# A 13-tile closing of a third half layer, with finer copies and new places, in a product-interaction MLP kernel

## The reference, cut to what matters

```python
sparse_embed = emb_tables[field_idx[None, :], x_sparse]   # 1024 x 26 x 64, gathered rows
z = sparse_embed.reshape(B, 26 * 64)
gram = jnp.einsum('bik,bjk->bij', sparse_embed, sparse_embed)
inner = gram[:, iu, ju]                                   # the 325 products of pairs of fields
dnn_in = jnp.concatenate([x_dense, z, inner], axis=-1)    # 13 + 1664 + 325 = 2002 columns
h = jax.nn.relu(dnn_in @ w1 + b1)                         # w1 is 2002 x 2002
out = jax.nn.sigmoid(h @ w2 + b2)
```

## Time and profile before

| | |
|---|---|
| median of 3 runs | 435.78 us (435.40 to 436.06) |
| the profiled execution | 435.87 us, of it the span from first to last instruction 434.1 us |
| TensorE busy | 409.5 us, 94% of the span |
| VectorE, ScalarE, GpSimd busy | 72%, 61%, 53% |
| TensorE's granted clock, mean | 0.992 of full speed |
| HBM read | 77.55 MB, 179 GB/s |

### The profile page before, as it was taken

One profiled execution on the slowest core, in us unless ns is written; L12 is line 12 of the kernel. 1 busy time (PEld: TensorE's weight loads), 2 busy tenths in 40 slices (PEclk: granted clock), 3 DMA queues, 4 the chain that ended last, 5 costly groups with the idle time before them and its releaser, 6 DMA issues.

```text
span 434.1 us, 5915 instructions
## 1 busy us (share of the span) xinstructions
PE 409.5 (94%) x1959; PEld 336.8 (78%) x1959; DVE 313.7 (72%) x691; ACT 265.2 (61%) x365; POOL 228.7 (53%) x215
## 2 busy tenths in 40 slices
PE   8769999899799999999999899989999999999996
PEld 8647878788678787888877778868888888778884
DVE  3374876586949987895998799995484986984432
ACT  3442363577996896967478595694952686353310
POOL 5777777877777877787787778781000000000000
PEclk9998999999899999999999999999999999999999
DMA  5787777775469776469699656686477157578400
GB/s 137 200 266 168 234 190 226 218 245 129 110 157 232 199 216 166 120 150 215 177 206 308 149 111 168 166 279 193 114 221 282 47 192 184 161 228 281 136 0 0
DMA packets 29454, 77.95 MB, mean 180 GB/s; under 512 B 8480, under 2 KB 8488, under 8 KB 29424
## 3 DMA queue, kind: packets, MB, share of 16 engines
q1 hardware_dynamic: 22768, 70.75, 51.6%
q0 software_dynamic: 6656, 6.83, 13.4%
HBM read 77.55 MB, written 0.00 MB: 179 GB/s over the span
## 4 chain that ended last, share of the span: by engine, by line
PE 52%; DVE 13%; POOL 12%; ACT 10%; issue 7%; DMA 4%; SPq 1%; DVEq 0%; ACTq 0%; POOLq 0%
PE ps L588 15%; PE ps L600 15%; PE ps L590 15%; POOL z L480 12%; PE ps L548 6%; ACT w_hi L668 3%; ACT pair_v L692 2%; DVE weighed L886 2%; DVE tail L844 2%; DVE w_lo L782 2%; DMA z<-in_L_rec_emb_tables_dram,idx 2%; DMA w_raw<-in_L_rec_w_dram 2%; ACT pair_u L689 2%; DVE square L825 1%; PE ps L534 1%
## 5 line engine op out<-in xcount | busy, mean ns | idle before, releaser
L480 POOL DMA_INDIRECT z<-in_L_rec_emb_tables_dram,idx x208 | 227.7, 1095 | 65.2 <-issue 62.5
L588 PE MATMUL ps<-w_hi,x_hi 128*128 128x502 f32 (+1 forms) x512 | 206.5, 403 | 7.9 <-DVE x_lo L790 4.6
L590 PE MATMUL ps<-w_lo,x_hi 128*128 128x502 f32 (+1 forms) x480 | 188.4, 393 | 0.0
L668 ACT CAST w_hi<-w_raw 128x1002 fp32r<-128x1002 f32 x128 | 128.7, 1033 | 49.4 <-PE ps L600 32.7
L600 PE MATMUL ps<-w_hi,x_lo 128*128 128x502 f32 (+1 forms) x480 | 139.8, 393 | 1.0 <-DVE x_lo L854 1.0
L588 PEld LDWEIGHTS ps<-w_hi,x_hi 128*128 128x128 f32 x512 | 97.2, 190 | 33.1 <-DVE x_lo L790 5.9
L600 PEld LDWEIGHTS ps<-w_hi,x_lo 128*128 128x128 f32 x480 | 90.3, 190 | 19.7 <-DVE x_lo L854 1.6
L590 PEld LDWEIGHTS ps<-w_lo,x_hi 128*128 128x128 f32 x480 | 91.6, 191 | 16.4
L782 DVE TENSOR_TENSOR w_lo<-w_raw,w_hi 128x1002 fp32r<-128x1002 f32 x60 | 70.1, 1198 | 26.3 <-ACT w_hi L668 26.1
L778 DVE TENSOR_TENSOR w_lo<-w_raw,w_hi 128x502 fp32r<-128x502 f32 x60 | 40.8, 680 | 28.7 <-ACT w_hi L668 28.5
L676 ACT CAST x_hi<-ps 128x256 fp32r<-128x256 f32 (+3 forms) x38 | 17.1, 450 | 52.5 <-PE ps L534 52.4
(11 more groups left out here) (51 smaller groups left out, 205.4 us busy)
## 6 DMA issues: line engine op xcount, KB each, us to landing
w_raw<-in_L_rec_w_dram SPq DMA_DIRECT2D x112, 501.0 KB
w_raw<-in_L_rec_w_dram SPq DMA_DIRECT2D x24, 250.5 KB
w_raw<-in_L_rec_w_dram SPq DMA_DIRECT2D x8, 438.4 KB
z<-in_L_rec_emb_tables_dram,idx POOLq DMA_INDIRECT x208, 4.4
w_raw<-in_L_rec_w_dram SPq DMA_DIRECT2D x24, 62.6 KB
w2b<-in_L_rec_w_dram SPq DMA_DIRECT2D x1, 501.0 KB, 5.9
w2b<-in_L_rec_w_dram SPq DMA_DIRECT2D x1, 500.0 KB, 7.1
w_raw<-in_L_rec_w_dram SPq DMA_DIRECT2D x8, 50.9 KB
```

The lines of the kernel that those rows point to most:

```text
L480: pool.indirect_dma_start(out=z[:, t % 2, K * f:K * (f + 1)], out_offset=None, in_=emb_rows, in_offset=bass.IndirectOffsetOnAxis(ap=idx[:, ...
L588: nc.tensor.matmul(into(c, t), hi, of_w(w_hi, c, k), start=first, stop=False)
L590: nc.tensor.matmul(into(c, t), hi, of_w(w_lo, c, k), start=False, stop=False)
L668: nc.scalar.copy(high_of(n), raw(n)).then_inc(w_hi_done, 1)
```

## The change

It does these things.

- The third pair's first half (pair 2, half 0) joins `SPLIT`: closed after its 13 z tiles, and its tail becomes one turn behind k 10 of its second half.
- 20 fillers at the start for 29; single fillers behind turns 3 and 98 for two behind turn 33.
- The low parts of weights are made in 4 instructions for the first pair (`W_PARTS`), 2 for the second, 1 for the others; before, 2, 2, 1, 1.
- The pair copies of a tile are four blocks with places of their own, for two; each block has the same instructions for one of the two `par`.
- Indices of the first four fields of the first two tiles are made first, the rest of these in a second round.
- Of tile 2 one block of products less is read by ScalarE and of tile 3 one more, and for tile 7 block 3 in place of block 2 (`BY_ACT`).
- Nearly all events have new places; those that the text speaks of stand below.

```diff
-    PARTS_OF = [(0, 7), (7, FP - 7)]
+    PARTS_OF = [(0, 0, 7), (1, 0, 7), (0, 7, FP - 7), (1, 7, FP - 7)]
...
-    WARM_UP = 29
+    WARM_UP = 20
+    W_PARTS = (4, 2, 1, 1)
...
-    TAIL_AFTER = {(1, 0, 9): [(0, 1)], (1, 0, 11): [(0, 0)], (2, 0, 2): [(1, 0)]}
-    SPLIT = [(1, 0)]
+    TAIL_AFTER = {(1, 0, 9): [(0, 1)], (1, 0, 11): [(0, 0)], (2, 0, 2): [(1, 0)], (2, 1, 10): [(2, 0)]}
+    SPLIT = [(1, 0), (2, 0)]
...
-        ('J', 0): [-1.0, -0.5, 0.0, 1.0, 2.0, 3.5, 5.2, 6.0, 7.5, 10.9, 14.3, 15.8, 18.4, 19.1, 19.2],
-        ('J', 1): [24.5, 26.3, 28.4, 31.5, 33.2, 36.4, 37.2],
-        ('O', 0): [13.4, 23.8],
-        ('G', 0): [25.8, 25.9, 26.6, 26.9],
-        ('R', 0): [27.9],
-        ('X', 0): [29.4],
-        ('O', 1): [27.7, 28.5],
+        ('J', 0): [-1.0, -0.5, 0.0, 1.0, 2.0, 5.2, 6.0, 7.5, 7.9, 10.9, 14.3, 15.4, 18.4, 19.6, 19.8],
+        ('J', 1): [24.0, 26.3, 28.4, 31.5, 33.0, 36.4, 37.2],
+        ('O', 0): [9.0, 16.1, 23.6, 23.6],
+        ('G', 0): [25.8, 25.9, 26.6, 26.7],
+        ('R', 0): [27.2],
+        ('X', 0): [29.8],
+        ('O', 1): [27.7, 27.7, 28.3, 28.5],
...
-        ('G', 2): [40.0, 40.8, 41.2, 41.4],
-        ('X', 2): [44.0],
-        ('T', 4): [44.8, 46.6, 48.5, 52.8],
-        ('T', 5): [53.3, 53.9, 57.2, 59.2],
-        ('X', 5): [70.0],
-        ('X', 7): [102.4],
+        ('G', 2): [40.0, 40.6, 41.1, 42.1],
+        ('X', 2): [45.3],
+        ('T', 4): [44.4, 47.3, 49.2, 53.5],
+        ('T', 5): [52.1, 53.8, 56.7, 58.7],
+        ('X', 5): [78.6],
+        ('X', 7): [99.8],
...
-    WARM = [(33.4, 2)]
+    WARM = [(3.5, 1), (98.5, 1)]
...
-                first, n = PARTS_OF[q]
+                par, first, n = PARTS_OF[q]
...
-            make_rows(slice(0, GROUP), idx_in, 0)
+            make_rows(slice(0, GROUP), slice(0, 2 * ALONE), 0, idx_in, 0)
+            make_rows(slice(0, GROUP), slice(2 * ALONE, FIELDS), GROUP * 2 * ALONE, idx_in, 3)
...
-                    if TURN[PIECE[m][0]][2][0] < GROUP * EARLY_PAIRS:
-                        half = CW[0]
-                        nc.vector.tensor_tensor(low[:, 0:half], raw(n)[at, 0:half], high[:, 0:half], ALU.subtract)
-                        nc.vector.tensor_tensor(low[:, half:], raw(n)[at, half:], high[:, half:],
-                                                ALU.subtract).then_inc(w_lo_done, 1)
+                    part = W_PARTS[TURN[PIECE[m][0]][2][0] // GROUP]
+                    if part > 1:
+                        ends = [HW * j // part for j in range(part + 1)]
+                        for lo, hi in zip(ends, ends[1:]):
+                            last = nc.vector.tensor_tensor(low[:, lo:hi], raw(n)[at, lo:hi], high[:, lo:hi], ALU.subtract)
+                        last.then_inc(w_lo_done, 1)
```

More of the change, by code:

```diff
@@ L175, in product_interaction_mlp_kernel @@
+        ('G', 6): [79.7, 81.3, 87.7, 88.0],
+        ('R', 6): [94.0],
+        ('X', 6): [97.2],
+        ('T', 7): [73.9, 75.1, 78.2, 90.7],
+        ('O', 7): [89.7, 91.0, 91.0, 91.4],
+        ('G', 7): [93.5, 94.5, 95.9, 96.5],
+        ('R', 7): [96.9],
+        ('X', 7): [99.8],
     }
-    WARM = [(33.4, 2)]
+    WARM = [(3.5, 1), (98.5, 1)]
     KINDS = "JTOGRXW"
@@ L487, in _ @@
                 if pair == 1:
-                    pool.wait_ge(idx_done, 2)
+                    pool.wait_ge(idx_done, 3)
                 for q, (first, n, of) in enumerate(JOINT[pair]):
+                    if pair == 0 and first == ALONE:
+                        pool.wait_ge(idx_done, 2)
                     if pair:
@@ L684, in pair_operands @@
                 act.wait_ge(x_hi_done, count("JTX", slices_event(t, first + n - 1)))
-                for par in range(2):
-                    high = x_hi[K * par:K * (par + 1), t % XS, first:first + n, :].rearrange(
-                        "p f (g b) -> p f g b", b=2)
-                    at, to = QUAD // 2 * par + first, FP * par + first
-                    nc.scalar.copy(pair_u[0:K, :, :, at:at + n, :].rearrange(two), high)
-                    if t in ACT_COPIES:
-                        nc.scalar.copy(pair_v[K:2 * K, :, :, to:to + n, :].rearrange(two), high)
-                    last = nc.scalar.mul(pair_v[0:K, :, :, to:to + n, :].rearrange(two),
-                                         high.bitcast(fp32), 0.5)
+                high = x_hi[K * par:K * (par + 1), t % XS, first:first + n, :].rearrange(
+                    "p f (g b) -> p f g b", b=2)
+                at, to = QUAD // 2 * par + first, FP * par + first
+                nc.scalar.copy(pair_u[0:K, :, :, at:at + n, :].rearrange(two), high)
+                if t in ACT_COPIES:
+                    nc.scalar.copy(pair_v[K:2 * K, :, :, to:to + n, :].rearrange(two), high)
+                last = nc.scalar.mul(pair_v[0:K, :, :, to:to + n, :].rearrange(two),
+                                     high.bitcast(fp32), 0.5)
                 last.then_inc(pairs_act, 1)
@@ L746, in _, with make_rows @@
         def _(dve):
-            def make_rows(tiles, loaded, step):
+            def make_rows(tiles, fields, first, loaded, step):
                 dve.wait_ge(loaded, 16)
-                i, w = idx[:, tiles, :], wrap[:, tiles, :]
+                i = idx[:, tiles, fields]
+                n = (tiles.stop - tiles.start) * (fields.stop - fields.start)
+                w = wrap[:, first:first + n].rearrange("p (t f) -> p t f", t=tiles.stop - tiles.start)
                 nc.vector.tensor_scalar(w, i, 0, VOCAB, ALU.is_lt, ALU.mult).then_inc(idx_step, 1)
```

64 lines of the change are left out of this document (28 added, 36 removed).

## The result

The changed kernel took 430.09 us in the median of 4 runs (428.32 to 431.55), the kernel before 435.59 beside it (435.24 to 436.06): a ratio of 0.9864, 95% interval 0.9827 to 0.9902. The forecast was 429.3, within 423.5 to 434.6. The profiled execution took 430.07 us, its span 428.3 for 434.1. Medians and ranges here are of all runs of a kernel; the ratios, each against the kernel before run beside it, leave out a run that is over 1.5% above the fastest of its kernel (one each in experiments 3, 5 and 7).

What follows compares the result with a forecast made beforehand. No one engine was taken to set the time: TensorE has half the chain and is held at a list of waits. 435.87 - 3.0 (up to G(1,0)) - 3.6 (five later waits) = 429.3 us, range 423.5 to 434.6.

Steps and rivals of the forecast that it cites:

- Fillers, 0: At the start: fewer fillers gain 0, since TensorE next waits for tile 1's first copy, behind weights; clock cost taken as 0.
- J(0,5), 2.0 ahead at turn 6: J(0,5) moved from behind turn 3 to behind turn 5: turn 6 starts at 36.0 for 38.0, 2.0 us ahead.
- Quarters, 2.9 off the gathers: First pair's low parts in four instructions: gather excess halves from 5.7, saving 2.9 us at the last gather, bounds 0 and 4.
- J(0,14), no wait: J(0,14) moved within turn 20: its 1.4 us wait for the last gather goes, 3.4 us ahead at turn 21.
- Indices in two rounds: At the start: the first gather comes 0.1 to 0.2 us earlier, nothing on the path by itself.
- ScalarE at turn 30, 3.0 ahead at G(1,0): 81 to 121 us: the tail's wait becomes a wait for ScalarE's copies; 3.0 us ahead at G(1,0).
- Five waits, 3.6: 121 to 430 us: five TensorE waits lose their cause, 2.82 us idle plus 0.165 each for pipelining, 3.6 us.
- The split, its own cost 0: Third pair's first half: four sums kept on ScalarE and added on VectorE are covered, cost 0; without that cover 2.7 us.
- The gathers hold: Rival, 10%: VectorE's instruction length does not delay gathers, the last lands at 80.5, lead 1.6 at G(1,0); 430.7 us.
- More of the list goes: Rival, 17%: as many waits again vanish and the start keeps 2 us more; 423.7 us.
- The lead is given back: Rival, 15%: from 100 to 290 us new places make new waits on ScalarE and VectorE; 433 us.
- ScalarE's order at turn 30: Rival, 8%: if the start gives nothing, turn 30 ends at 121.8, 0.9 late; 437.5 us; decides below 0.7 lead at turn 26.

Runs made afterwards that it cites:

- experiments 3, 5 and 7: 3: kernel before with the start's changes, 431.47 us; 5: that plus split and three tile-6 places, 429.16; 7: changed kernel, T(5) places back, 430.91, or all corrections, 431.50.
- experiment 1: The changed kernel with the first pair's low parts of weights in two instructions again (halves) instead of four: 432.91 us, ratio 0.9942.
- experiment 3: The start alone: the kernel before with the change's fillers, quarters, indices in two rounds and J(0) places, the rest as before: 431.47 us, ratio 0.9901.
- the three places more: The kernel before with the change's start, the split, and tile 6's pair copies earlier and products later: 429.16 us, ratio 0.9858.
- J(1,2) ahead: The changed kernel with J(1,2), tile 1's low tail, placed ahead of the third and fourth blocks of tile 1's pair copies: 430.78 us, ratio 0.9874.
- experiments 6 and 7: Profiles with fillers: 6, the changed kernel with ten fillers ahead of turn 30, 430.63 us; 7, all five corrections in one kernel, those fillers included, 431.50 us.

## Why the prediction was right, step by step

The time came out 0.8 us above the forecast, within what a measurement can tell: the interval of the ratio is 1.6 us to either side, not the 0.9 that I had assumed. Of the sum, the first term was 3.0 and measured 3.44 (lead at G(1,0)); the second was 3.6 and measured 2.37 (5.81 less 3.44). Not all that fits fits for the reason given: in both terms errors of opposite sign made up for one another, and that is luck.

**Fillers, 0.** Right up to J(0,8), and the risk was real: the clock did fall behind 16.50. With 29 fillers it does not, and J(0,8)'s gather takes the difference back, but the clock then falls behind that gather. (The price read from rows 3 comes to 2.5 - 0.79 = 1.7, not 1.6.)

**J(0,5), 2.0 ahead at turn 6.** The direction was right, the size too small: turn 6 started at 34.25, not 36.0. Turn 4 started at 27.80 where I had 29.05, since turn 3 ended earlier, not 0.6 later; and turn 6 waited 0.55 us, 0.8 with the pipelining, less than my lower bound of 1.2. What I missed is the other half of the same line of places: J(0,8) within turn 8 waits 1.22 for its gather and takes 1.1 of the 3.7 back.

**Quarters, 2.9 off the gathers.** The excess is 2.5 us where I had 2.9 left of 5.7, and putting halves back restores it. "Half the length, half the excess" was right within what the gathers vary (2.1 to 3.5 us of excess in ten of eleven profiles with quarters, 4.7 to 5.7 in three with halves). The last gather landed at 76.26, not at 77.6, since it also took less from issue to landing (6.29 us for 7.63). What the step missed is that early gathers and those of later pairs stood close to the path too (experiment 1).

**J(0,14), no wait.** Right: 77.84 follows its neighbours. The lead was 4.6, not 3.4, since the step before it was too small.

**Indices in two rounds.** The first gather started at 3.86, not earlier than before (3.83). Nothing, as priced, but not even the 0.1.

**ScalarE at turn 30, 3.0 ahead at G(1,0).** The order of events was right: the tail's wait gone, ScalarE's copy in its place, the clock down. The instant of G(1,0), foreseen at 117.5 and come at 117.44, is luck. The lead at turn 21 was 1.2 larger than I had, and it did arrive: turn 30 started at 112.61 for 113.6, and the last pair copy ended at 116.33 for 117.5. The fall of the clock in turn 30, of which I had put in about half, took 1.1 back. The new places of tiles 0 and 1 brought nothing to it (experiment 3).

**Five waits, 3.6.** Here the sum was wrong inside and near right outside. Gone without a successor: 173.55, 284.01 and 379.14. Near the wait at 190.64 there are waits of 0.61 and 0.21 now, at 186.20 and 187.56. The wait at 239.07 stayed, 0.58 for 0.62. That T(5) holds the E sums' banks was right; that an earlier place on TensorE frees them was not. T(5,3) is transposed at 226.72, but its copies come at 234.23 and 235.66, behind tile 4's pair copies and two tiles of weights on ScalarE and VectorE, and the bank is free only then. And the other moves, priced at nothing with a bound of +2, were a loss: from G(1,0) to turn 69 the lead fell by 0.8, where the old places, behind the same start, raised it by 0.8 in experiment 3. Behind turn 69 the lead rose by 3.1, where the two waits priced there made 1.64. That the second term came within 1.3 us is luck: two of its five waits and the other moves fell short, and the split brought more than its price.

**The split, its own cost 0.** Cost 0 held, and it brought more than the 1.19 of X(5)'s wait: 2.0, since the second layer's stops at the end of that half went too. What the step left out is its condition: the split brings forward tile 6's products, and without new places for them it brings nothing (1.0002).

**The rivals.** *The gathers hold* is refuted by the halves, and with it what I drew from the Trainium skill (SBUF — State Buffer, Who interferes with whom) for these gathers; the part of its rule on GpSimd's reads may cover them (experiment 1). *More of the list goes* did not come. *The lead is given back* came in part, 1.9 us between turns 21 and 69, of which 1.1 went to the clock in turn 30 and 0.8 to waits behind it; the split made it good. *ScalarE's order at turn 30* was a true mechanism with the wrong condition: the start gave 4.6 us, far above the 0.7 at which it decides.

## What to carry to other kernels

While GpSimd's gathers are on the path, cut VectorE's long instructions beside them: the same subtraction in four parts cost 0.3 us more a piece and gave about 3 us. A lead passes through a stretch in which another engine is busy 95% of the time, as ScalarE was here (3.8 us at turn 21 and at G(1,0) in the start alone), since that engine runs earlier by it too. But no further lead is won there by moving or removing single waits on TensorE, which only moves its idle time; work has to leave that engine without making the next one late. When a stage is shortened, move the copies ahead of the next stage by as much, or its first consumer takes the gain.

## What was not expected of the hardware

TensorE's granted clock falls to the lower of its two levels (1.2 for 2.4 GHz) for some 3.4 us in most profiles, mostly behind idle time of TensorE, but at instants that one can't read off the idle time. In the start alone no fall came behind 1.50 and 1.56 us of idle time at 112 and 117; with the three places more, 1.75 and 1.59 at nearly the same places were followed by a low clock of almost 7 us; with halves it fell at 102.4, when TensorE had done transposes and blocks of pair products with 0.39 us of idle time among them; with J(1,2) ahead, the clock was low for most of the first turns:

```profile
12.00:23.00 11.00, 8.67 (x22) 6.45 (x23) 4.65 (x14) 4.47 (x7) 8.46 (x9) 0.53 0.79 181
```

At the low level matmuls start 0.42 us apart for 0.226, so 3.4 us hold 8 of them and lose 8 x 0.19, 1.6 us. That is more than most of the edits tried here are worth. Fillers in or behind the idle time kept the clock up near turn 30 in both profiles with them (experiments 6 and 7), but where ScalarE's copies hold the next step, only a part of the 1.6 comes back.
